# Selective scan: GpSimd takes the drive of every second slot and eleven of sixteen output products

## The reference

```
dt, B, C = split(u @ x_proj_w.T); dt = softplus(dt @ dt_proj_w.T + dt_proj_b)
A = -exp(A_log)                                  # 512 channels x 32 states
def step(h, (ut, dtt, Bt, Ct)):                  # over 128 time steps
    dA = exp(dtt[..., None] * A)
    h = dA * h + dtt[..., None] * Bt[:, None, :] * ut[..., None]
    y = einsum('bdn,bn->bd', h, Ct)
    return h, y
y = ys + u * D                                   # then gated by silu(z), projected by out_proj_w
```

## Time and profile before

| | |
|---|---|
| median of 3 runs | 1187.06 us (1186.12 to 1187.51) |
| the profiled execution, its own time | 1188.65 us |
| the profiled execution, its span | 1186.9 us |
| the scan's loop, first scan to last product | 1050.29 to 1109.04 us |
| TensorE busy in the span | 96% |
| VectorE, ScalarE, GpSimd busy | 76%, 76%, 49% |

### The profile page before, as it was taken

The page is one execution under the profiler, slowest core; times in us unless marked ns, Lnnn a source line. Parts: engine busy times, 40 slices in busy tenths (PEclk is TensorE's granted clock), DMA queues, the critical chain, the costliest instruction groups (busy, mean ns, idle before and its releaser), DMA issues.

```text
span 1186.9 us, 32392 instructions
## 1 busy us (share of the span) xinstructions
PE 1137.4 (96%) x12680; PEld 806.6 (68%) x12681; DVE 901.6 (76%) x1710; ACT 901.5 (76%) x1550; POOL 586.8 (49%) x548
## 2 busy tenths in 40 slices
PE   3899999999999999999999999999997899989998
PEld 1466666666666666666666666666666758767898
DVE  6687877887888888888878788878775699788622
ACT  4499989888898988888888888988885268687010
POOL 6155656565666656566656565656555070043000
PEclk8899999999999999999999999999999999999999
DMA  5256554535454545454545454444442994150284
GB/s 217 64 160 184 131 149 95 152 89 155 92 151 92 156 93 148 94 141 106 134 110 139 106 130 117 123 121 92 125 93 91 363 346 149 61 178 1 100 287 176
DMA packets 141285, 163.56 MB, mean 138 GB/s; under 512 B 18336, under 2 KB 127296, under 8 KB 141136
## 3 DMA queue, kind: packets, MB, share of 16 engines
q1 hardware_dynamic: 140592, 159.43, 48.0%
q10 hardware_dynamic: 544, 2.10, 0.5%
HBM read 71.86 MB, written 12.99 MB: 71 GB/s over the span
## 4 chain that ended last, share of the span: by engine, by line
PE 82%; DVE 8%; DMA 3%; issue 3%; ACT 2%; SPq 1%; POOL 0%; DVEq 0%; ACTq 0%; POOLq 0%
PE ps L872 20%; PE ps L844 20%; PE ps L909 7%; PE ps L885 7%; PE ps L2290 4%; PE ps L926 4%; PE ps L928 4%; PE ps L927 4%; PE ps L1615 3%; DMA k_st<-k_rest 2%; PE ps L2298 2%; PE ps L2072 2%; PE ps L2054 1%; PE ps L1066 1%; PE ps L894 1%
## 5 line engine op out<-in xcount | busy, mean ns | idle before, releaser
L468 POOL TENSOR_TENSOR pT_lo<-p_exp,pT_hi 128x896 f16<-128x896 f32 x223 | 421.2, 1889 | 324.4 <-ACT pT_hi L568 324.4
L549 ACT ACTIVATE p_exp<-ps,ln_k,esc 128x896 f32<-128x896 f32 x224 | 246.3, 1100 | 53.8 <-PE ps L909 45.8
L681 DVE TENSOR_REDUCE tile_max<-ps 128x128 f16<-128x896 f32 x224 | 244.4, 1091 | 49.5 <-PE ps L885 47.2
L568 ACT ACTIVATE pT_hi<-p_exp 128x896 f16<-128x896 f32 x224 | 211.9, 946 | 1.0
L676 DVE TENSOR_TENSOR v_lo<-ps,v_hi 128x512 f16<-128x512 f32 x196 | 135.5, 691 | 76.8 <-ACT v_hi L541 74.4
L872 PE MATMUL ps<-c_hi,wk_hi 128*128 128x448 f16 x448 | 159.3, 356 | 6.0 <-DVE c_lo L663 4.8
L927 PE MATMUL ps<-v_lo,pT_hi 128*128 128x64 f16 x1568 | 164.4, 193 | 0.0
L926 PE MATMUL ps<-v_hi,pT_hi 128*128 128x65 f16 x1568 | 164.3, 193 | 0.1
L928 PE MATMUL ps<-v_hi,pT_lo 128*128 128x65 f16 x1568 | 163.8, 193 | 0.0
L872 PE MATMUL ps<-c_lo,wk_hi 128*128 128x448 f16 x448 | 158.8, 354 | 0.0
L872 PE MATMUL ps<-c_hi,wk_lo 128*128 128x448 f16 x448 | 158.6, 354 | 0.0
(11 more groups left out here) (402 smaller groups left out, 2073.7 us busy)
## 6 DMA issues: line engine op xcount, KB each, us to landing
k_st<-k_top SPq DMA_DIRECT2D x444, 112.0 KB, 2.3
k_st<-k_rest SPq DMA_DIRECT2D x444, 56.0 KB, 2.0
c_raw<-in_ctxT SPq DMA_DIRECT2D x14, 896.0 KB, 5.7
xa_cn<-in_ctx SPq DMA_DIRECT2D x14, 896.0 KB, 8.1
me_w<-in_me_w SPq DMA_DIRECT2D x8, 1536.0 KB, 6.4
ctx_parts<-c_hi SPq DMA_DIRECT2D x14, 448.0 KB, 3.0
ctx_parts<-c_lo SPq DMA_DIRECT2D x14, 448.0 KB, 3.0
me_w<-in_me_w SPq DMA_DIRECT2D x8, 768.0 KB, 5.9
```

Of the source, the lines that this page charges most:

```text
L468: nc.gpsimd.tensor_tensor(pT_lo[:, n % 2, :, :].rearrange("p t s -> p (t s)"), p_exp[:, n % 2, :], pT_hi[:, n % 2, :, :].rearrange("p t s ...
L549: nc.scalar.activation(p_exp[:, n % 2, :], s_scores[n % 2], ACT.Exp, bias=ln_k[:, 0:1], scale=esc[:, n // H0 % 2:n // H0 % 2 + 1]).then_in ...
L568: nc.scalar.activation(pT_hi[:, n % 2, :, :].rearrange("p t s -> p (t s)"), p_exp[:, n % 2, :], ACT.Copy).then_inc(pT_hi_ready, 1)
L681: nc.vector.tensor_reduce(tile_max[:, n % 2, :], s_scores[n % 2].rearrange("p (t s) -> p s t", s=S), AX.X, ALU.max).then_inc(tile_max_done, 1)
```

## The change

- Odd slots: the drive is made by GpSimd as an elementwise product `b_all` x `du` into a new SBUF tile `drv` (two slots of it). `b_all` holds the 8 rows of B of slots 1 and 3 (of each group the odd slots use states 8 to 15 and 24 to 31) on all partitions, by two broadcast transfers that stand ahead of c_all's four. TensorE makes the drives of even slots alone; scan q of an odd slot reads both its inputs from SBUF.
- Two of the four diagonals remain: slot 0's on VectorE, slot 2's on GpSimd.
- Even slots have the four PSUM banks to themselves, so a drive waits for scan q-4, in place of q-2. GpSimd's drive waits for scan q-4 too.
- `POOL_READS` grows from seven to eleven slots; VectorE keeps products 2, 6, 10, 14 and 15.
- GpSimd's order becomes: diagonal 2, drive 1, drive 3, and for each group j: product 4j, product 4j+1, drive 4j+5, product 4j+3, drive 4j+7.
- Products wait for all four transfers of c_all; `c_wait`, which let every group's first slot go on after the first of them, is gone. B's rows pass through DRAM with C's (64 rows in place of 32).
- TensorE turns group 1's du before sum 0, and issues drive q+4 behind sum q.

```diff
-POOL_READS = (1, 3, 5, 7, 9, 11, 13)
+POOL_READS = (0, 1, 3, 4, 5, 7, 8, 9, 11, 12, 13)
...
-        bd, c_all = t("bd", [S, NS, S]), t("c_all", [P, NS, S])
+        bd, c_all = t("bd", [S, 2, QS, S]), t("c_all", [P, NS, S])
+        b_all, drv = t("b_all", [P, 2, QS, S]), t("drv", [P, 2, QS, S])
...
-        bc_dram = nc.dram_tensor("ss_bc", [NS, S], F32).ap()
+        bc_dram = nc.dram_tensor("ss_bc", [2 * NS, S], F32).ap()
...
         def slot(q):
-            return ps[:, 2 * (q % 2):2 * (q % 2) + 2, :].rearrange("p b n -> p (b n)")
+            if on_pool(q):
+                return drv[:, q // 2 % 2, :, :].rearrange("p n s -> p (n s)")
+            return ps[:, 2 * (q // 2 % 2):2 * (q // 2 % 2) + 2, :].rearrange("p b n -> p (b n)")
...
-            sp.dma_start(bc_dram, dbl[RANK + NS:, :]).then_inc(E["c_passed"], 16)
+            sp.dma_start(bc_dram, dbl[RANK:, :]).then_inc(E["c_passed"], 16)
             sp.wait_ge(E["c_passed"], 16)
+            for k in range(2):
+                lo, hi = states(2 * k + 1)
+                sp.dma_start(b_all[:, k, :, :], bc_dram[lo:hi, :].rearrange("(o n) s -> o n s", o=1).to_broadcast([P, QS, S])).then_inc(E["c_passed"], 16)
             for q in range(NS // QS):
...
-            for q in range(1, NS // QS):
-                drive_diagonal(nc.gpsimd, q)
-            for q in POOL_READS:
+
+            def drive(q):
+                j, k = q // 4, q // 2 % 2
+                pool.wait_ge(E["c_passed"], 48)
+                pool.wait_ge(E["du_ready"], min(j, 2) + 1)
+                at_least(pool, E["scanned"], q - 3)
+                nc.gpsimd.tensor_tensor(drv[:, k, :, :], b_all[:, k, :, :], du[:, j, :].unsqueeze(1).to_broadcast([P, QS, S]),
+                                        ALU.mult).then_inc(E["pool_driven"], 1)
+
+            def read(q):
                 lo, hi = states(q)
                 hs = h[:, q // 4 % 2, lo:hi, :]
-                c_wait(pool, q)
+                pool.wait_ge(E["c_loaded"], NS // QS * 16)
                 pool.wait_ge(E["scanned"], q + 1)
                 nc.gpsimd.tensor_tensor(hs, hs, c_all[:, lo:hi, :], ALU.mult).then_inc(E["pool_read"], 1)
+
+            pool.wait_ge(E["du_ready"], 1)
+            drive_diagonal(nc.gpsimd, 2)
+            drive(1)
+            drive(3)
+            for j in range(CT):
+                read(4 * j)
+                read(4 * j + 1)
+                if j + 1 < CT:
+                    drive(4 * j + 5)
+                    read(4 * j + 3)
+                    drive(4 * j + 7)
...
                 v.wait_ge(E["decay_ready"], q + 1)
-                v.wait_ge(E["driven"], q + 1)
+                v.wait_ge(E["pool_driven" if on_pool(q) else "driven"], q // 2 + 1)
...
-                at_least(pe, E["scanned"], q - 1)
+                at_least(pe, E["scanned"], q - 3)
...
             turn(first)
             drive(0)
-            drive(1)
+            drive(2)
+            turn(second)
             for q in range(NQ):
                 j = q // 4
-                if q + 2 < NQ:
-                    drive(q + 2)
                 add_up(q)
-                if q == 0:
-                    turn(second)
                 if q == 4:
                     turn(rest)
+                if q % 2 == 0 and q + 4 < NQ:
+                    drive(q + 4)
                 if q % 4 == 3 and j:
                     project(j - 1)
             project(CT - 1)
```

More of the change, by code:

```diff
@@ L1733, in selective_scan @@
                                          "dt_done", "parts_ready", "raw_ready", "dt_ready", "du_ready", "c_passed",
-                                         "c_loaded", "uD_ready", "bd_ready", "decay_ready", "driven", "scanned", "read", "pool_read",
+                                         "c_loaded", "uD_ready", "bd_ready", "decay_ready", "driven", "pool_driven", "scanned", "read", "pool_read",
                                          "summed", "y_ready")}
         PARTS = len(LOG1P) + 1
[L1738 to L1743, removed]
         def u_bank(j):
@@ L1764, in states, with on_pool @@
             return q * QS % NS, q * QS % NS + QS
+        def on_pool(q):
+            return q % 2 == 1
         def slot(q):
-            return ps[:, 2 * (q % 2):2 * (q % 2) + 2, :].rearrange("p b n -> p (b n)")
+            if on_pool(q):
+                return drv[:, q // 2 % 2, :, :].rearrange("p n s -> p (n s)")
+            return ps[:, 2 * (q // 2 % 2):2 * (q // 2 % 2) + 2, :].rearrange("p b n -> p (b n)")
         def drive_diagonal(engine, q):
             lo, hi = states(q)
-            engine.tensor_tensor(bd[:, lo:hi, :], ident[:, :].unsqueeze(1).to_broadcast([S, QS, S]),
+            engine.tensor_tensor(bd[:, q // 2, :, :], ident[:, :].unsqueeze(1).to_broadcast([S, QS, S]),
                                  bT[:, lo:hi].unsqueeze(2).to_broadcast([S, QS, S]), ALU.mult).then_inc(E["bd_ready"], 1)
@@ L1781, in _ @@
             sp.wait_ge(E["x_copied"], 1)
-            sp.dma_start(bc_dram, dbl[RANK + NS:, :]).then_inc(E["c_passed"], 16)
+            sp.dma_start(bc_dram, dbl[RANK:, :]).then_inc(E["c_passed"], 16)
             sp.wait_ge(E["c_passed"], 16)
+            for k in range(2):
+                lo, hi = states(2 * k + 1)
+                sp.dma_start(b_all[:, k, :, :], bc_dram[lo:hi, :].rearrange("(o n) s -> o n s", o=1).to_broadcast([P, QS, S])).then_inc(E["c_passed"], 16)
             for q in range(NS // QS):
                 lo, hi = states(q)
-                sp.dma_start(c_all[:, lo:hi, :], bc_dram[lo:hi, :].rearrange("(o n) s -> o n s", o=1).to_broadcast([P, QS, S])).then_inc(E["c_loaded" if q else "c_passed"], 16)
+                sp.dma_start(c_all[:, lo:hi, :], bc_dram[NS + lo:NS + hi, :].rearrange("(o n) s -> o n s", o=1).to_broadcast([P, QS, S])).then_inc(E["c_loaded"], 16)
             me.load_first(sp)
@@ L1800, in _ @@
                 nc.gpsimd.tensor_scalar(uD[:, j, :], u[:, j, :], cols[:, C_DPAR + j:C_DPAR + j + 1], None, ALU.mult).then_inc(E["uD_ready"], 1)
-            pool.wait_ge(E["du_ready"], 1)
-            for q in range(1, NS // QS):
-                drive_diagonal(nc.gpsimd, q)
-            for q in POOL_READS:
+            def drive(q):
[6 more added lines that the diff above has]
+            def read(q):
                 lo, hi = states(q)
                 hs = h[:, q // 4 % 2, lo:hi, :]
-                c_wait(pool, q)
+                pool.wait_ge(E["c_loaded"], NS // QS * 16)
                 pool.wait_ge(E["scanned"], q + 1)
                 nc.gpsimd.tensor_tensor(hs, hs, c_all[:, lo:hi, :], ALU.mult).then_inc(E["pool_read"], 1)
+            pool.wait_ge(E["du_ready"], 1)
[9 more added lines that the diff above has]
+                    drive(4 * j + 7)
         @block.scalar
@@ L1960, in _ @@
                 if q not in POOL_READS:
-                    c_wait(v, q)
+                    v.wait_ge(E["c_loaded"], NS // QS * 16)
                     v.wait_ge(E["scanned"], q + 1)
@@ L2047, in drive @@
             def drive(q):
-                j, (lo, hi) = q // 4, states(q)
+                j = q // 4
                 pe.wait_ge(shared["turned_copied"], min(j, 2) + 3)
                 if j == 0:
-                    pe.wait_ge(E["bd_ready"], q + 1)
-                at_least(pe, E["scanned"], q - 1)
+                    pe.wait_ge(E["bd_ready"], q // 2 + 1)
+                at_least(pe, E["scanned"], q - 3)
                 for k in range(2):
                     mm = nc.tensor.matmul(slot(q)[:, 512 * k:512 * k + 512], duT[:, j, :],
-                                          bd[:, lo + 4 * k:lo + 4 * k + 4, :].rearrange("p n s -> p (n s)"), start=True, stop=True)
+                                          bd[:, q // 2 % 2, 4 * k:4 * k + 4, :].rearrange("p n s -> p (n s)"), start=True, stop=True)
                 mm.then_inc(E["driven"], 1)
```

## The result

| | before | changed |
|---|---|---|
| median | 1186.59 us (1184.47 to 1187.51, 4 runs) | 1198.36 us (1196.86 to 1200.85, 4 runs) |
| ratio | | 1.0104, 95% interval 1.0079 to 1.0128 |
| the profiled execution, its own time | 1188.65 us | 1197.11 us |
| first scan to the end of the last product | 58.7 us | 71.7 us |
| last product's end to the start of the last addition | 3.2 us | 3.3 us |

The change makes the kernel 11.8 us slower by the medians (the ratio in the table is a little larger than that of the two medians, 1.0099); forecast were 13. The two profiled executions differ by only 8.5 us, because the changed one happened to reach the scan stage 4.7 us earlier, through code that the change doesn't touch (its first scan starts at 1045.63 us, 1050.29 before).

A forecast was written before the change was run, and what follows sets the result against it. TensorE was taken to bound the scan stage at 3.51 us a slot, then turns shared by VectorE and GpSimd. Later scan 4 +4.1, the rest of the loop +7.9, clock +1: +13.0, forecast 1200.0 us, range 1195 to 1206.

The forecast's parts named there:

- TensorE is the bound and leaves it: Scan stage: TensorE bounds at 3.51 us a slot; with 8 drives gone, some 44 us stay and it bounds no longer.
- Scans with two SBUF inputs are excluded like the others: Odd slots' scans, reading decay and drv from SBUF, take turns with GpSimd: 8 at 2.13 us, 17.1 us.
- The two that wait go by who asked first: VectorE and GpSimd instructions that exclude each other in the scan stage are served first come, first served.
- The ledger, not below 67.3 us: Scan stage: GpSimd and VectorE instructions that must go one after another total 67.3 us from 1050.0 us, a floor of +8.3.
- Scan 4 comes 4.1 us later: Start of scan stage: held step-size instructions and product 2's wait move scan 4 from 1064.66 to 1068.8 us.
- From scan 4 on, 52.3 us: From scan 4's start to product 15's end: 52.3 us where it was 44.4, that is +7.9.
- The parts named beside these two: Waits listed for +4.1 and +7.9: step-size instructions held some 2.2 or 2.0 each, product 2's 2.1, 16.5 per four-slot group.
- The clock, +1: TensorE's idle 1110.0 to 1114.5 us slows sums 12 and 13, delaying the last sums: 0 to 3 us, taken as 1.
- The sum: Whole kernel: +4.1 + 7.9 + 1 = +13.0 us, forecast 1200.0 us.
- That nothing is excluded: Rival, scan stage: GpSimd bounds with 46.5 us of work and last sums end 5 us earlier, 1182 us; chance 0.08.
- that odd scans are not: Rival: only products and step sizes are excluded; last sum 0 to 6.5 us later, 1187 to 1194 us; chance 0.12.
- That TensorE stays slow: Rival: TensorE stays at 1.2 GHz in the scan stage, a group costs 22 us, some 1212 us; chance 0.04.

The follow-up runs named there:

- experiment 1: The changed kernel, but odd slots' scans read a stale even slot in PSUM instead of drv (output wrong): 1192.70 us, 1.0052 of the kernel before.
- experiment 5: The kernel before, but all 16 scans read their second input from an SBUF tile instead of PSUM (output wrong): 1198.15 us, 1.0107.
- experiment 9: experiment 8 plus step size's accumulator in PSUM and GpSimd's list in another order: 1186.17 us, 0.9999 of the kernel before.
- experiment 4: The changed kernel with dummy matmuls in TensorE's four idle stretches: 1199.48 us, 1.0109 of the kernel before.
- experiment 8: The changed kernel, but ScalarE copies each drv to PSUM for the odd scans, with TensorE's drives ordered as before: 1194.93 us, 1.0077 of the kernel before.
- experiment 10: experiment 9 with product 8 also on VectorE and TensorE's drives 8, 10, 12, 14 behind sums 4, 6, 8, 10: 1181.32 us, 0.9959 of the kernel before.

## Why the prediction was right

- *TensorE is the bound and leaves it.* Right. From 1070 to 1101 us it is now busy 20.7 of 31 us (30.9 in the earlier trace rows), and the chain runs over GpSimd.
- *A drive on GpSimd costs 2.35 us.* Right: the first two, undisturbed, took 4.70.
- *Scans with two SBUF inputs are excluded like the others.* No row of before showed it; it carried 17.1 of the 67.3 us of the ledger. Experiments 1 and 5 show it from both sides: 5.9 us of the loop come back when it is taken away (less than 17.1, since other waits then bound), 12.7 come when it is put into the kernel before. The sign given, odd scans above 2.28 us, came true for four of the eight. What the Trainium skill states (SBUF — State Buffer, "SBUF: two separate sides") for any VectorE op with two SBUF inputs holds for the scan in this trace: 4.23 us instead of 2.28.
- *The two that wait go by who asked first.* Right, as in the zip at 1097 us; experiment 9 shows the price of a wrong guess. The prices held as well: a held drive ended 2.15 us after the scan (2.23 were reckoned), a held product 1.08 after GpSimd.
- *The ledger, not below 67.3 us.* From the start of drive 1 to the end of product 15 it took 70.5 us, 3.2 above the floor.
- *Scan 4 comes 4.1 us later.* Mis-sized. It starts 19.7 us after scan 0, 14.4 before: +5.3. Three small instructions of the second step size were held (by 1.2, 2.1 and 2.1 us), not two. B's rows took 5.1 us from issue to landing instead of 4.1, behind a copy to DRAM of 1.8 us instead of 1.4, so that drive 1 started 1.2 us after scan 0 and not 0.3 before it.
- *From scan 4 on, 52.3 us.* 52.0 measured, against 44.4 before: +7.7 where 7.9 was forecast.
- *The parts named beside these two.* They don't add up to them: 2 x 2.2 + 2.1 - 1.5 is 5.0 and not 4.1, and 2 x 2.0 with three groups at 1.8 is 9.5 and not 7.9. The totals are those of the layout, and the text doesn't say which waits swallow the difference; so the path is right, but these two sums can't be followed from the text.
- *Behind the last product, nothing.* 3.3 us against 3.2.
- *The clock, +1.* Wrong in size and place, the one term whose mechanism failed: it fell in the first idle stretch as said, and then before sums 4 and 8, not 12. It delayed scan 12 by 1.45 us, not the last sums, and in experiment 4, with the clock at 1.00, the loop is as long: it was worth less than 0.1 us.
- *The sum.* Loop and what follows it: forecast +12.0 and 1 for the clock, measured +13.1. The median moved by 11.8; the interval (9.4 to 15.2 us) holds both. That the sum fits to 0.1 us is luck: scan 4 came 1.2 us later than forecast, and the clock's 1 us was not there.
- *The rivals.* That nothing is excluded, and that odd scans are not, fall with experiments 1 and 5. That TensorE stays slow falls with the changed kernel's own trace: its clock is 1.00 from 1059 to 1070 us and from 1101 to 1117. (The price given for it is a slip: 4 x 22 against 4 x 14.67 is 29.3 us more, some 1216.)

What stays open: the loop of the one trace and the median of all runs don't always move alike. Against the kernel before, they differ by up to 2.1 us, either way: experiment 8 is 7.9 us slower by its loop and 8.9 by its median, experiment 9 is 2.0 faster and 0.2 slower (0.5 us of this lies between its last product and the addition), experiment 10 is 3.8 and 5.6 faster. Medians of the kernel before moved by 1.1 us between the groups of runs (1186.0 to 1187.1). Differences of 1 or 2 us between two of these kernels should not be read closer than that.

## What to carry to other kernels

Before moving elementwise work from VectorE or TensorE to GpSimd, list not the busy times but the instructions on both engines that have to take turns: VectorE's with two inputs in SBUF, GpSimd's that read SBUF. Add up their lengths as if they were one engine's; here that gave 67 us against a loop of 59 before, though GpSimd alone needed 46.5, and the loop came out at 71.7. Where the result of GpSimd's work is VectorE's second input, its place matters: a copy to PSUM by ScalarE (1.0 us for 1024 columns; ScalarE was busy 39 of the loop's 58.7 us before, so it had room) took 5.0 us off the loop (the loss is 0.77% in place of 1.04%), and together with the accumulator in PSUM and the new lists it became a gain of 0.41%. Short chained VectorE instructions beside long GpSimd ones are the dearest for their length: one of 0.3 us can be held for 2.1.

## What the runs showed of the hardware that was not expected

- A wait removed beside a shared turn tends to come back as another one. Keeping TensorE warm took away a wait of 1.45 us and changed the loop by less than 0.1 us; taking 7.2 us of holding off the small instructions gained 3.2.
- Which of two instructions asks first by a tenth or two of a us decides who is held: VectorE's product 10 took 3.33 us when drive 13 was 0.11 us ahead of it (experiment 9), and 1.30 when it was itself 0.18 ahead (experiment 10), with the drive at 3.34.
- TensorE at half clock in three stretches of the changed kernel cost less than 0.1 us of the loop, since what it was late for would have waited for GpSimd instead.
